# Moving the sum of a softplus from VectorE to GpSimd in a state-space and expert kernel

## What is computed

```
dt = softplus(xn @ dt_w.T + dt_b)                 # [token, 256]
A  = -exp(log_A);  b = xn @ B_w.T + B_b;  c = xn @ C_w.T + C_b     # 32 states
h  = exp(A * dt) * h + (dt * xn) * b              # scan over the 1024 tokens
y  = sum over states(h * c) + D_skip * xn
out = x + y + moe(xn)                             # 8 experts, best 2 of each token
```

## Time and profile before

| | |
|---|---|
| median of three runs | 3823.92 us |
| profiled execution, its own time | 3817.81 us |
| its span | 3816.1 us |
| VectorE busy | 3647.8 us, 96% |
| GpSimd busy | 3261.9 us, 85% |
| TensorE busy | 3229.2 us, 85% |
| ScalarE busy | 2564.6 us, 67% |
| granted clock, mean | 0.977 |

### The profile page before, as it was taken

The page is one execution under the profiler, slowest core; times in us unless marked ns, Lnnn a source line. Parts: engine busy times, 40 slices in busy tenths (PEclk is TensorE's granted clock), DMA queues, the critical chain, the costliest instruction groups (busy, mean ns, idle before and its releaser), DMA issues.

```text
span 3816.1 us, 64710 instructions
## 1 busy us (share of the span) xinstructions
PE 3229.2 (85%) x16548; PEld 2095.9 (55%) x16548; DVE 3647.8 (96%) x2281; ACT 2564.6 (67%) x4811; POOL 3261.9 (85%) x1722
## 2 busy tenths in 40 slices
PE   7776888888888888888888888888888888888887
PEld 4354555555555555555555555555555555555554
DVE  7787999999999999999999999999999999999998
ACT  3245677677776777767676767767676677767775
POOL 0017999999998999999998999999999999999996
PEclk9888999999999999999999999999999999999999
DMA  9975555555656556555656556465656555565555
GB/s 327 341 115 150 162 163 160 174 144 145 169 163 179 168 150 173 153 153 162 164 165 179 164 153 157 136 180 156 170 162 180 163 159 136 147 191 158 165 169 163
DMA packets 345305, 645.57 MB, mean 169 GB/s; under 512 B 49405, under 2 KB 221441, under 8 KB 344641
## 3 DMA queue, kind: packets, MB, share of 16 engines
q1 hardware_dynamic: 252018, 538.77, 43.8%
q0 software_dynamic: 67776, 85.24, 14.1%
q10 hardware_dynamic: 25104, 16.91, 2.0%
HBM read 515.55 MB, written 142.80 MB: 173 GB/s over the span
## 4 chain that ended last, share of the span: by engine, by line
issue 30%; DVE 25%; POOL 18%; PE 12%; ACT 7%; DMA 6%; DVEq 1%; POOLq 1%; SPq 1%; ACTq 0%
DVE hc L1214 12%; POOL u L1026 11%; DVE h L1225 10%; PE bank L639 3%; POOL out_rows L985 3%; PE bank L648 3%; ACT bank L798 2%; POOL xg L973 2%; DMA dt<-x 2%; DMA dt<-dt_rows 2%; PE bank L494 2%; ACT xgt L802 1%; POOL dtx_n L958 1%; ACT ht L840 1%; DMA bc_rows<-bcv 1%
## 5 line engine op out<-in xcount | busy, mean ns | idle before, releaser
L1026 POOL TENSOR_TENSOR u<-dtx,b_sb 128x1024 f32<-128x1024 f32 x1024 | 2514.5, 2523 | 146.1 <-DVE h L1225 102.7
L1225 DVE TENSOR_TENSOR_SCAN h<-bank,u 128x1024 f32<-128x1024 f32 x1024 | 2300.2, 2276 | 27.6 <-ACT bank L798 15.5
L798 ACT ACTIVATE bank<-dt,a_neg 128x1024 f32<-128x1024 f32 x1026 | 1129.0, 1108 | 401.7 <-DVE h L1225 309.7
L639 PE MATMUL bank<-xgt,w_sb 128*128 128x256 f32 x4096 | 1045.7, 400 | 257.3 <-ACT ht L840 216.6
L1214 DVE TENSOR_TENSOR hc<-h,bank 128x2048 f32<-128x2048 f32 x514 | 1163.6, 2264 | 44.9 <-ACT bank L868 44.3
L639 PEld LDWEIGHTS bank<-xgt,w_sb 128*128 128x128 f32 x4096 | 756.9, 195 | 636.7 <-issue 551.4
L648 PE MATMUL bank<-w_sb,ht 128*128 128x256 f32 x4096 | 936.4, 382 | 29.1 <-ACT o_sb L855 29.1
L648 PEld LDWEIGHTS bank<-w_sb,ht 128*128 128x128 f32 x4096 | 763.0, 191 | 221.4 <-issue 128.7
L840 ACT ACTIVATE ht<-bank,b_sb 128x256 f32<-128x256 f32 x1024 | 423.0, 463 | 288.4 <-PE bank L639 288.4
L598 PE MATMUL bank<-hc,rsum 128*32 128x512 f32 x4112 | 551.0, 608 | 2.5 <-DVE hc L1214 2.5
L985 POOL DMA_INDIRECT out_rows<-o_sb,sidx x258 | 415.4, 1610 | 55.6 <-issue 36.2
(11 more groups left out here) (114 smaller groups left out, 1821.9 us busy)
## 6 DMA issues: line engine op xcount, KB each, us to landing
b_sb<-bc_rows SPq DMA_DIRECT2D x258, 512.0 KB, 4.1
c_sb<-bc_rows SPq DMA_DIRECT2D x258, 512.0 KB, 4.2
dt<-dt_rows SPq DMA_DIRECT2D x132, 512.0 KB, 7.6
dtx<-dtx_rows SPq DMA_DIRECT2D x132, 512.0 KB, 5.2
w_sb<-w SPq DMA_DIRECT2D x18, 1024.0 KB, 7.7
dt_rows<-dt_n SPq DMA_DIRECT2D x137, 128.0 KB, 3.9
dtx_rows<-dtx_n SPq DMA_DIRECT2D x137, 128.0 KB, 1.8
out_rows<-y_sb POOLq DMA_DIRECT2D x34, 512.0 KB, 6.7
```

Source lines behind the costliest of these rows:

```text
L639: mm = pe.matmul(m_ps[:, c, :], w1_sb[:, kk, ch * P:(ch + 1) * P], xgt[:, kk, :], start=(kk == 0), stop=(kk == KD - 1))
L798: act.activation(a_ps[k % 2], dt[:, k % GPP, :], ACT.Exp, scale=a_neg[:, col:col + 1]).then_inc(a_ready, 1)
L1026: pool.tensor_tensor(u[:, k % UB, :], dtx[:, gp, :], b_sb[:, j, :], ALU.mult).then_inc(u_ready, 1)
L1225: dve.tensor_tensor_scan(h[:, k, :], a_ps[k % 2], u[:, k % UB, :], 0.0, ALU.mult, ALU.add).then_inc(scan_done, 1)
```

## The change

GpSimd adds the two parts of dt in place of VectorE. Since it has no way to PSUM, the logarithm is written into SBUF, into `za`, and the sum comes behind the first `u` of the following step. ScalarE takes max(z, 0) and |z| straight from PSUM, in four instructions in place of two and one. The logarithm moves from k = 6 to k = 4, and `c_copy(0)` from k = 7 to k = 6. The semaphore `za_done` and the PSUM view `zl_ps` go. In the part ahead of the loop VectorE still adds, from SBUF, but for the last slice, which GpSimd takes in its first step.

```diff
 def evac_z(p):
     act.wait_ge(dt_done, p + 1)
     for g in range(KD):
-        ins = act.activation(zv[:, g, :], z_ps[:, g * Q:(g + 1) * Q], ACT.Identity, bias=dtb[:, g:g + 1])
+        act.activation(zv[:, g, :], z_ps[:, g * Q:(g + 1) * Q], ACT.Relu, bias=dtb[:, g:g + 1])
+        ins = act.activation(za[:, g, :], z_ps[:, g * Q:(g + 1) * Q], ACT.Abs, bias=dtb[:, g:g + 1])
     return ins
 def softplus(p):
-    act.activation(za[:], zv[:], ACT.Abs).then_inc(za_done, 1)
-    act.wait_ge(za_done, p + 1)
     act.activation(ze[:], za[:], ACT.Exp, scale=-1.0).then_inc(ze_done, 1)
 def log_part(p):
     act.wait_ge(ze_done, p + 1)
-    act.activation(zl_ps, ze[:], ACT.Ln, bias=1.0).then_inc(l_done, 1)
+    act.activation(za[:], ze[:], ACT.Ln, bias=1.0).then_inc(l_done, 1)
...
 def c_copy(i):      # in the branch of i == 0
-    act.wait_ge(dt_done, p + 2)
+    act.wait_ge(hc_done, 4 * st + 5)
...
     softplus(p)
+    log_part(p)
     c_copy(3)
 if k == 6:
     down_out(0)
-    act.wait_ge(hc_done, 4 * st + 5)
-    log_part(p)
+    c_copy(0)
 if k == 7:
-    c_copy(0)
     down_out(1)
     lay_scatter()
...
+def dt_part(p):
+    pool.wait_ge(l_done, p + 1)
+    pool.wait_ge(dt_st, 16 * p + 1)
+    pool.wait_ge(prep_done, p + 1)
+    settle(pool)
+    pool.tensor_tensor(dt_n[:], zv[:], za[:], ALU.add).then_inc(dt_done, 1)
...
     add_y((hf + 2 * B - 2 + ng - 1) % (2 * B), ng - 1)
+if k == 0:
+    dt_part(NG + 1 + st)
 if k < SJ:
     gather(st + 1, (s + 1) % 2, k)
...
-    prep_dt(NG + 2 + st)      # VectorE, behind the last scan of a step
```

More of the change, by code:

```diff
@@ L169, in ssm_moe @@
         bc_ps = bank[0:2 * N, 6, KD * Q:(KD + 1) * Q]
-        zl_ps = bank[:, 6, KD * Q:2 * KD * Q].rearrange("p (k t) -> p k t", k=KD)
         turn_ps = bank[:, 6, :].rearrange("p (k s) -> p k s", s=SL)
@@ L241, in ssm_moe @@
         v_done = sem("v_done")
-        za_done = sem("za_done")
         ze_done = sem("ze_done")
@@ L614, in _ @@
             pe.wait_ge(map_ready, 1)
-            pe.wait_ge(dt_done, NG + 3)
+            pe.wait_ge(l_done, NG + 2)
             pe.wait_ge(xg_in, 16 * SJ)
@@ L1129, in prep_dt @@
                 dve.wait_ge(prep_done, p + 1)
-                dve.scalar_tensor_tensor(out=dt_n[:], in0=zv[:], scalar=0.0, in1=zl_ps,
-                                         op0=ALU.max, op1=ALU.add).then_inc(dt_done, 1)
+                dve.tensor_tensor(dt_n[:], zv[:], za[:], ALU.add).then_inc(dt_done, 1)
             tot = bank[:, 2:4, :].rearrange("p b c -> p (b c)").rearrange("p (i e) -> p i e", e=E)
@@ L1191, in _ @@
             prep_dt(NG)
-            prep_dt(NG + 1)
             dve.wait_ge(oh_used, 2 * NT // OHB + 2)
```

## The result

The changed kernel takes 3855.96 us (median of 4 runs, 3852.38 to 3861.19) against 3822.39 us for the kernel before (4 runs, 3820.14 to 3826.01). The ratio is 1.009, with a 95% interval of 1.0072 to 1.0107: 34 us slower, where 3829 us, no change, was forecast and 3845 us was the end of the range.

The account below looks back on a forecast made before the run. VectorE (96% busy) was taken as the bound, GpSimd close behind with 102.7 us in hand. GpSimd's sum 88.3 - waits 102.7 + unfilled waits 24 - end 4.6 = +5.0 us, so 3829 us, no change; range 3806 to 3845 us.

Parts of the forecast that it names:

- VectorE's sum goes: VectorE's queue: each step loses 0.31 us, the ordinary step becomes 26.26 us, 39.7 us less if nothing else is late.
- GpSimd's sum, 0.69 us: GpSimd's queue: the added sum costs 0.69 us a step, 88.3 us more over 128 steps (80.6 to 124).
- The balance: GpSimd: its 102.7 us of waits take in the 88.3 us; with every wait filled its path is 14.4 us shorter.
- The signs named for the forecast: GpSimd 87 to 88% busy, u waiting 20 to 40 us for scans, VectorE's ordinary step 26.2 to 26.6 us, among others.
- In ordinary steps the sum hardly waits for the logarithm: GpSimd, ordinary steps: first u ends 2021.83, logarithm about 2023.2; stores push GpSimd 1.5 us back beyond that; priced at nothing.
- Waits that can't be filled: GpSimd at eight long sequence starts: second u 2.6 us later, 3.0 us of waits remain each, 24 us (0 to 40).
- the long boundaries: Eight of fifteen sequence boundaries: the seven where weights are reloaded and one more; the one timed takes 32.55 us.
- 3 to 5 us shorter: The other seven of fifteen sequence boundaries, said to be some 3 to 5 us shorter than the eight long ones.
- how much of that comes through depends on the load of `dt`, which starts behind GpSimd's `u`: Long boundaries: GpSimd some 5 us less ahead, so other engines reach them relatively earlier; 2 us taken, 3.0 us remain.
- ScalarE's two more passes, 0.52 us ahead of the third copy of c: ScalarE in evac_z: gains 0.52 us ahead of that copy, loses 0.45 us behind it; at 67% busy not the bound.
- The earlier copy of c, uncounted: Sequence starts: earlier c_copy(0) removes a wait of VectorE, uncounted as GpSimd doesn't wait for it.
- Rival A: Long boundaries: sum's wait for the logarithm stays whole, 5.0 us in each of eight blocks; +25.6 us, 3849 us; chance 0.34.

Follow-up runs that it names:

- traffic added alone: Fastest kernel of the study plus one more 1 MB HBM-to-HBM copy in each sequence's last step, which only SyncE waits for: 3819.0 us, 0.9983.
- Moving the `dt` loads: Changed kernel with second and third dt loads issued ahead of the last dtx and second b load in each half sequence's last step: 3822.03 us, 1.0007.
- two columns: Changed kernel with GpSimd's sum cut to one of each 128 columns, the wait for the logarithm kept: 3848.91 us, 1.0073.
- the late sum with two passes: Changed kernel with the sum behind the third u, z leaving the bank in two passes, absolute value and relu taken later in SBUF: 3797.69 us, 0.9946.
- the fastest kernel: Changed kernel with the sum behind the third u, z leaving the bank in two passes, and the dt loads issued earlier: 3782.98 us, 0.9903.
- the kernel before with the dt loads first: Kernel before with only the dt loads moved ahead in SyncE's queue: 3807.63 us, 0.9947.

## Why the prediction was wrong

*VectorE's sum goes:* right. The ordinary step is 26.24 us, as forecast to 0.02.

*GpSimd's sum, 0.69 us:* right. Where it never waits (behind the third `u`) its record is 0.71 to 0.74 us, and in an ordinary step of the changed kernel the queue is 6.09 - (2022.00 - 2016.59) = 0.68 us longer.

*The balance:* right. The added work costs nearly nothing by itself (1.001). The signs named for the forecast came as well: GpSimd at 87% of the span, its `u` waiting 25.3 us for scans, the ordinary step at 26.24 us. They could not tell, since the loss lay at the boundaries, with TensorE.

*"In ordinary steps the sum hardly waits for the logarithm: priced at nothing":* this is the step that failed. The working had found that the first `u` ended at 2021.83 and the logarithm at about 2023.2, and wrote the 1.4 us off, since stores would push GpSimd further back. It counted waits as lost time of GpSimd, of which there was enough. But a wait in GpSimd's queue for something ScalarE does late in each step is a cap on the lead, and the lead had a use: it decides when `u` frees `dtx`, when SyncE's queue moves and when the loads end. The waits seen in steps other than the second of a sequence are only 21 us in all, but GpSimd's lead at the last step of the sequences was 5.2 us for 7.8 us and the last load of `dtx` went out 6.0 us ahead of the last scan for 7.6 us. That the wait's place and not the work makes the loss of 0.9% is shown by cutting the sum (1.0073), leaving it out (1.0072), moving it by one `u` (1.001) and adding the work alone (1.001). How it gets from the late loads to VectorE is shown in part: TensorE's return stalls longer (3.37 us for 1.83), its clock is at the lower level for 6.4 us for 2.1, and traffic added alone does the same (+31 us). Moving the `dt` loads (1.0007) proves little of it, as they gave 0.53% in the kernel before as well. Why TensorE's instructions come late stays open.

*"Waits that can't be filled", 24 us in eight blocks:* wrong in place and size. Only the long boundaries were priced. The seven with weights lost 6.7 us; the eight without, of which seven were dismissed as "3 to 5 us shorter", lost 27.6 us. Those seven were short because TensorE's return stall was 1.3 to 2.1 us there and its clock stayed full in five of them, and that was what the change used up. The sum's wait, put at 2.6 us in eight blocks, is 3.3 us in all fifteen. The sentence "how much of that comes through depends on the load of `dt`, which starts behind GpSimd's `u`" named the link and then took 2 us for it in the wrong direction: the boundary didn't come earlier for GpSimd.

*ScalarE's two more passes, 0.52 us ahead of the third copy of c, uncounted as ScalarE is busy 67%:* wrong, 18 us. At places 1 and 5 ScalarE waits for TensorE's z, and the step grew by 0.51 and 0.71 us there: no slack ahead of that copy.

*TensorE:* in no sum of the prediction. Its clock and its return to the loop's start were left at what they were.

*The earlier copy of c, uncounted:* right, nothing.

*Rival A* (3849 us) had the right neighbourhood by the wrong way: it charged the wait to GpSimd's own path, and the runs with two columns and without the sum, in which GpSimd had time to spare, were as slow.

In ratios, the changed kernel's loss is then the cap (0.9%) and the passes (0.5%) against what VectorE's 40 us leave. Without both (the late sum with two passes) the gain is 0.54%, not 1.0%; 0.43% more comes with the earlier dt loads, but 0.53% came with these in the kernel before as well. So of the fastest kernel's 37 us some 17 belong to the moved sum. Where the rest of VectorE's 40 us goes is not settled; places 1, 4 and 5 (0.61, 0.16 and 0.48 us over the free step of 26.24) and the starts hold it, and no run took them apart.

## What to carry to other kernels

An instruction that is moved to an engine with idle time brings its waits along: ask how far ahead that engine runs and what its lead releases, and put the instruction behind enough other work that what it waits for is ready even at full lead. An engine's average load tells nothing of the slack at one spot of its queue, so price extra passes by what stands behind them there. Look at the boundaries that are short now, since they are short thanks to something that can be lost. And where TensorE pauses longer than before, read the granted clock of the stretch behind the pause: in step 24 the slow matmuls cost twice what the longer pause did.

## What the runs showed of the hardware

- VectorE's sum of 128x256 takes 0.40 us with one operand in PSUM and 1.37 to 1.49 us on the mean with both in SBUF beside GpSimd's `u`; single ones took 3.6 us and ended with the `u`. The Trainium skill ("SBUF — State Buffer", SBUF: two separate sides) has this rule: a VectorE operation with two SBUF inputs and a GpSimd one that reads SBUF exclude each other for the whole instruction. The trace agrees, and the kernels with such a sum were 2.3 and 2.7% slower.
- A wait in GpSimd's queue set where the gather behind it came: 1.3 us behind the end of ScalarE's logarithm, with a sum of two columns as with none, however long the `u` ahead had been over.
- TensorE's return to the start of its loop took from 0.9 us (in the kernel before with the dt loads first) to 5.7 us (with 1 MB of extra traffic). It ended about 2 us behind the end of a 16 KB packet of instructions, which itself took about 1 us.
- In step 24 of the changed kernel TensorE's granted clock fell from 1.00 to 0.50 while the engine stood still for 3.65 us, and stayed there for 10 us, in which it worked with gaps; eight matmuls then took 3.40 to 3.75 us for 1.97.
